# A cross-attention and expert block on one core: a new order of the same instructions on every engine, and a new bank table

## The reference

```python
# attention, on the normalised x
q = proj(_layernorm(x), Wq, bq); k = proj(ctx, Wk, bk); v = proj(ctx, Wv, bv)
scores = clip(einsum('bhsd,bhtd->bhst', q, k) / sqrt(32), -50, 50)
scores = clip(where(attend, scores, -10000.0), -50.0, 50.0)
probs = softmax(scores)
ctx = einsum('bhst,bhtd->bhsd', probs, v)
delta = clip(residual_scale, 0, 0.3) * (ctx @ Wo.T + bo)
x = x + layernorm(delta) * ln_gamma + ln_beta
# experts, on the normalised new x
logits = einsum('bth,eh->bte', _layernorm(x), router_w)
gate = softmax(logits) * top2_mask
h = silu(einsum('bth,eih->beti', _layernorm(x), down_w))
x = x + einsum('beth,bte->bth', einsum('beti,ehi->beth', h, up_w), gate)
```

## Time and profile before

| | us |
|---|---|
| median of 3 runs | 198.33 (197.42 to 199.66) |
| the profiled execution, device time | 198.77 |
| its span, first to last instruction | 197.1 |
| PE busy in it | 178.3 (90%) |
| DVE, ACT, POOL busy | 143.6, 112.5, 104.5 |
| mean granted clock of PE | 0.963 |

### The profile page before, as it was taken

The page is one execution under the profiler, slowest core; times in us unless marked ns, Lnnn a source line. Parts: engine busy times, 40 slices in busy tenths (PEclk is TensorE's granted clock), DMA queues, the critical chain, the costliest instruction groups (busy, mean ns, idle before and its releaser), DMA issues. The chain is left out here.

```text
span 197.1 us, 3587 instructions
## 1 busy us (share of the span) xinstructions
PE 178.3 (90%) x1228; PEld 130.7 (66%) x1228; DVE 143.6 (73%) x306; ACT 112.5 (57%) x231; POOL 104.5 (53%) x157
## 2 busy tenths in 40 slices
PE   7999999399993999999599999986999999999970
PEld 7777686258832587885286876663775977888840
DVE  2867799999845894056982606789698999678991
ACT  3038537778309685175666833589554868567500
POOL 4060035499969999388694111794244872472000
PEclk9999999969998599999889999999999999999998
DMA  5994994005694326773305401553434482002337
GB/s 165 358 388 143 292 398 181 0 7 226 176 254 147 78 91 190 174 192 127 110 0 189 139 10 39 192 211 110 119 106 157 155 276 73 0 2 106 136 130 271
DMA packets 18050, 30.14 MB, mean 153 GB/s; under 512 B 3056, under 2 KB 8176, under 8 KB 17776
## 3 DMA queue, kind: packets, MB, share of 16 engines
q1 hardware_dynamic: 18032, 29.92, 46.6%
HBM read 19.95 MB, written 9.96 MB: 152 GB/s over the span
## 5 line engine op out<-in xcount | busy, mean ns | idle before, releaser
L471 PE MATMUL ps<-hst_hi,wq_hi 128*128 128x512 f32 x64 | 27.4, 428 | 0.0
L471 PE MATMUL ps<-hst_hi,wq_lo 128*128 128x512 f32 x64 | 26.4, 413 | 0.0
L471 PE MATMUL ps<-hst_lo,wq_hi 128*128 128x512 f32 x64 | 26.4, 412 | 0.0
L471 PE MATMUL ps<-wo_hi,attt_hi 128*128 128x512 f32 x64 | 26.1, 407 | 0.0
L471 PE MATMUL ps<-wo_hi,attt_lo 128*128 128x512 f32 x64 | 25.3, 395 | 0.0
L471 PE MATMUL ps<-wo_lo,attt_hi 128*128 128x512 f32 x64 | 25.2, 394 | 0.0
L1510 POOL TENSOR_TENSOR attt_lo<-wk,attt_hi 128x512 fp32r<-128x512 f32 x16 | 23.3, 1471 | 1.5 <-ACT attt_hi L802 1.5
L1506 POOL TENSOR_TENSOR xs<-xs,beta_bc 128x512 f32<-128x512 f32 x16 | 21.4, 1366 | 2.2 <-DMA beta_bc<-beta 2.2
L862 ACT ACTIVATE cen<-xs,n_sum 128x512 f32<-128x512 f32 x16 | 11.5, 721 | 15.5 <-DVE xs L1175 15.5
L1148 DVE TENSOR_SCALAR stage<-stage,exp_max 128x1024 f32<-128x1024 f32 x16 | 19.0, 1205 | 2.0 <-ACT stage L784 1.8
L765 ACT ACTIVATE hs<-xs,ln_bias,ln_rstd 128x512 f32<-128x512 f32 x16 | 12.1, 808 | 13.2 <-POOL ln_bias L1498 13.2
(11 more groups left out here) (111 smaller groups left out, 396.9 us busy)
## 6 DMA issues: line engine op xcount, KB each, us to landing
wk<-rz_scratch SPq DMA_DIRECT2D x32, 128.0 KB, 2.7
out<-xs SPq DMA_DIRECT2D x16, 256.0 KB, 2.3
xs<-x SPq DMA_DIRECT2D x3, 1024.0 KB, 7.8
x_scratch<-x_turned SPq DMA_DIRECT2D x6, 512.0 KB, 2.6
x_turned<-x_scratch SPq DMA_DIRECT2D x24, 128.0 KB, 2.7
hs_scratch<-hs_turned SPq DMA_DIRECT2D x2, 1024.0 KB, 3.8
hs<-hs_scratch SPq DMA_DIRECT2D x8, 256.0 KB, 5.2
wk<-wk_t SPq DMA_DIRECT2D x4, 256.0 KB, 5.9
```

The costliest lines, as they stand in the source:

```text
L471: last = pe.matmul(dst, w, m, start=start and i == 0, stop=stop and i == n - 1, skip_group_check=unseen)
```

## The change

No function is changed and no instruction is added or removed, but for how adjacent ones group: the calls in the blocks of SP, PE, ACT, DVE and POOL stand in another order, and `BANKS` has other lines. The order of the start (loads, keys, values, batch 0's `query`) stays. Of the bank table one line:

```diff
-    "V0 h11 s00 v01 m0 s10 v11 s20 v21 f00 f02 a00 v30 v33 f12 f21 n30 f30 a21 a31",
+    "V0 h11 m0 v01 s10 s11 v12 s20 f01 f02 v22 v30 a01 f10 f12 f21 n31 f23 n32 a21",
```

SP, from the first transfer after the loads:

```diff
-            hs_send(2)
             spread_out(0, 0)
             spread_in(0, 0)
-            hs_fetch(2)
-            load(3)
             spread_out(0, 1)
             spread_in(0, 1)
+            hs_send(2)
+            hs_fetch(2)
+            spread_out(1, 0)
+            load(3)
+            spread_in(1, 0)
+            spread_out(1, 1)
+            x1_send(0, 0)
+            spread_in(1, 1)
+            x1_fetch(0, 0)
             hs_send(3)
+            x1_send(0, 1)
             hs_fetch(3)
```

```diff
+            x1_transpose(3, 3)
+            up(2, 0)
+            down(3, 2)
+            up(2, 1)
             hid_transpose(2, 1)
-            x1_transpose(3, 3)
-            down(3, 2)
             down(3, 3)
-            up(2, 0)
-            up(2, 1)
             hid_transpose(3, 0)
             up(2, 2)
             up(2, 3)
+            up(3, 0)
             hid_transpose(3, 1)
-            up(3, 0)
```

DVE and POOL:

```diff
             centre_wo(0)
             centre_wo(1)
+            centre_wo(2)
             tile_stats(2, 0)
             tile_stats(2, 1)
-            scale_gamma()
             tile_stats(2, 2)
-            tile_stats(2, 3)
-            clip(0, 0)
             hs_lo(1, 0)
             hs_lo(1, 1)
             hs_lo(1, 2)
+            clip(0, 0)
+            hs_lo(1, 3)
+            tile_stats(2, 3)
             clip(0, 1)
...
+            batch_power(1)
             up_low()
-            batch_power(1)
+            wo_low(0)
+            wo_low(1)
             add_beta(0, 0)
             add_beta(0, 1)
-            batch_power(2)
             add_beta(0, 2)
             add_beta(0, 3)
             add_beta(1, 0)
+            batch_power(2)
+            wo_low(2)
             add_beta(1, 1)
             add_beta(1, 2)
```

More of the change, by code:

```diff
@@ L644, in _ @@
             hs_transpose(1, 2)
+            scores(0, 0)
             hs_transpose(1, 3)
+            expert_means()
             scores(0, 1)
+            query(1, 0)
             sums(0, 0)
[L648 removed]
             query(1, 1)
[L650 to L651 removed]
             sums(0, 1)
@@ L986, in _ @@
+            hs_hi(3, 3)
+            x1_out(0, 2)
+            projected_squares(1, 3)
             x1_squares(1, 2)
-            projected_squares(1, 3)
+            x1_out(0, 3)
+            exp_scores(2, 2)
+            down_scaled(0, 1)
+            hidden_tanh(0, 0)
+            x1_squares(1, 3)
+            exp_scores(2, 3)
+            query_out(3, 0)
+            x1_out(1, 0)
+            x1_out(1, 1)
+            query_out(3, 1)
+            down_scaled(0, 2)
+            exp_logits(0, 0)
@@ L1402, in _ @@
             x1_turn(1, 1)
+            clip(2, 1)
             scaled(1, 2)
             residual(1, 2)
+            scaled(1, 3)
+            reciprocals(2, 0)
+            x1_turn(1, 2)
+            residual(1, 3)
+            x1_turn(1, 3)
+            clip(2, 2)
+            clip(2, 3)
             product(2, 0)
             product(2, 1)
-            x1_turn(1, 2)
+            largest(0, 0)
+            gating(0, 0)
+            reciprocals(2, 1)
+            largest(0, 1)
+            gating(0, 1)
+            clip(3, 0)
+            clip(3, 1)
             product(2, 2)
-            scaled(1, 3)
-            residual(1, 3)
-            x1_turn(1, 3)
             product(2, 3)
-            clip(3, 0)
-            largest(0, 0)
-            clip(3, 1)
-            gating(0, 0)
             reciprocals(3, 0)
@@ L1419, in _ @@
             clip(3, 3)
-            largest(0, 1)
+            scaled(2, 0)
             hid_lo(0, 0)
-            reciprocals(3, 1)
-            scaled(2, 0)
-            residual(2, 0)
-            gating(0, 1)
-            scaled(2, 1)
-            residual(2, 1)
-            x1_turn(2, 0)
-            x1_turn(2, 1)
-            hid_lo(0, 1)
-            scaled(2, 2)
             product(3, 0)
             product(3, 1)
+            scaled(2, 1)
+            reciprocals(3, 1)
+            hid_lo(0, 1)
+            residual(2, 0)
+            x1_turn(2, 0)
+            residual(2, 1)
+            x1_turn(2, 1)
+            scaled(2, 2)
             residual(2, 2)
             x1_turn(2, 2)
+            scaled(2, 3)
             product(3, 2)
-            product(3, 3)
-            scaled(2, 3)
-            finish(0, 0)
             residual(2, 3)
@@ L1442, in _ @@
             largest(1, 0)
-            largest(1, 1)
+            product(3, 3)
+            finish(0, 0)
             finish(0, 1)
             finish(0, 2)
+            finish(0, 3)
             gating(1, 0)
+            largest(1, 1)
+            hid_lo(1, 0)
             gating(1, 1)
+            scaled(3, 0)
+            residual(3, 0)
             largest(2, 0)
-            finish(0, 3)
-            scaled(3, 0)
-            hid_lo(1, 0)
             hid_lo(1, 1)
-            residual(3, 0)
             gating(2, 0)
```

426 lines of the change are left out of this document (198 added, 228 removed), and 14 rows, old and new, of the table BANKS.

## The result

The changed kernel took **190.5 us** in the median of 4 runs (190.36 to 192.76), against 198.26 (197.42 to 199.66, 4 runs) for the kernel before: ratio 0.9629, 95% interval 0.9538 to 0.9719. The forecast was 190.5 us. The profiled execution took 190.64 us with a span of 188.8 us; the mean granted clock was 0.989, and 0.963 before. Executions that took over 1.5% more than the fastest of their kernel are left out of all medians, ranges and intervals here (for after_both these were four at 191.22 to 192.2 us with mean granted clocks of 0.98 to 0.986, while its other two had 1.0 and 0.998), and the profiles of after_two_stores and before_no_beta, which are of such executions, serve only to place waits.

A forecast was written before the change was run, and what follows sets the result against it. TensorE, busy 90% of the 197.1 us span, was taken as the bound. Removing 16.6 us of waits and clock loss gave 180.5; 8.7 of new waits made 189.2 of span, 190.5 us after run offsets; range 185.5 to 197.

The forecast's parts named there:

- The base: TensorE's old waits, 11.3 us, plus clock loss, 5.3 us: 16.6 us can go, leaving a floor of 180.5 us span.
- Place A: Batch-1 projection, TensorE waiting for hst_lo: 1.8 us (1.2 to 3.4) replaces 3.2 + 0.9; no clock loss.
- The clips: Three early VectorE clips, possibly delayed by GpSimd, hold weigh(0, 0): 0 to 2.0 us of wait, taken as 0.9.
- Place B: ScalarE held behind batch 2's DRAM transfer: 6.2 us go; the next late chain, reciprocals' broadcast, taken as 0 (0 to 2.0).
- The front of the projections: project(0, 0) waits for two GpSimd att_lo: 0 to 2.9 us, taken as 1.8 including weigh(1, 0)'s small wait.
- `weigh(3, 0)`: Batches 2 and 3: it waits for two products behind a 7.4 us reciprocal spread; 0 to 2.0, taken as 1.1 us.
- The end and the small waits: New alternation of the last up, hid_transpose and down: 1.2 us (0 to 2.5); other small waits 0.6.
- The tail: Last up, finish adds and stores, ending at 197.1 us: counted as something that can't go.
- (1): Rival: new waits hide one another, about a third of 8.7 us left; 184.7 us, chance 0.15.
- (2): Rival: waits at project(0, 0) or weigh(3, 0) pass some 2 us and lower the clock; about 194 us, chance 0.18.
- (3): Slower rival: reciprocal spreads through DRAM take 11 us or more and become the bound; about 203 us, chance 0.09.
- (4): Rival: clips and residuals meet GpSimd as often as before; 193 us, chance 0.08.

The follow-up runs named there:

- after_both: Changed kernel with the edits of after_lo_first and after_bo_late together; 188.27 us from two executions, no interval.
- after_two_stores: Changed kernel with each half's reciprocals stored to DRAM twice, one store behind the other; 196.56 us, ratio 0.9877 to the kernel before.
- before_no_beta: Kernel before without GpSimd's sixteen adds of ln_beta (ln_beta missing from the output); 195.92 us, ratio 0.9862 to the kernel before.
- after_lo_first: Changed kernel with batch 1's low parts on VectorE ahead of three of batch 2's statistics; 187.33 us, ratio 0.9471 to the kernel before.
- before_exp_first: Kernel before with query_out(1, 3) and batch 1's first two exponentials ahead of batch 2's four hs_hi on ScalarE; 200.18 us, ratio 1.0127.
- after_bo_late: Changed kernel with centre_bo moved behind product(0, 3) on VectorE; 189.44 us, ratio 0.953 to the kernel before.
- before_lift_lo: Kernel before with batch 1's low parts (VectorE) and tile (1, 3)'s high part (ScalarE) moved ahead of batch 2's steps; 200.87 us, ratio 1.0128.

## Why the prediction came out as it did

**The base was right.** The old stretch less the waits and clock of before is 184.1 - 16.6 = 167.5 us. The changed kernel's rows of waits give 8.4, and the lowered clock 1.5 (below): 177.4, which is what was measured. For after_lo_first, 167.5 and its rows of 1.8, 1.7, 1.3, 0.9, 0.9, 0.7, 0.5 and 0.3 us give 175.6, against 175.5. That the sum of waits plus clock accounts for PE's time held in both.

**Place A**: taken as 1.8 us, measured 2.44, inside its bounds but above the 1 to 2 us that the prediction named as its sign. "I take no clock loss here" failed. The `scores` took 2.01 for 1.11 us and `query(1, 0)` 3.64 for some 3.05 (43.34 to 46.98): 1.5 us. after_lo_first got both wait and clock back, 3.1 us, of which 1.9 are left in its stretch, as small waits of up to 1.0 us appeared elsewhere. The kernel's old order itself was uneven here: the same wait was 3.23 us in its profile and 1.65 in that of before_exp_first, which has the same steps up to there. In the second PE came 0.4 us later and DVE 1.2 us earlier, 0.9 of that by one `centre_wo` of 0.49 us in place of 1.42; why they differed stays open. The step on the clock rested on one counter-example, 1.6 us without a loss, for a wait whose own bound was 3.4.

**The clips**: 0.9 was taken at `weigh(0, 0)`, where it was 0: only one of the first four took over 1 us (1.14). The delay came one batch later, where no term stood: `clip(1, 0)` and `clip(1, 1)` took 3.45 us together beside GpSimd's `att_lo` and `wo_low`, and `sums(1, 0)` waited 1.40. The mechanism was right and its place wrong. after_bo_late took that wait away and had no shorter stretch, as the clock fell behind the next wait.

```profile
59.69 3.45 DVE L1148 TENSOR_SCALAR stage<-stage,exp_max 128x1024 f32<-128x1024 f32 x2
```

The Trainium skill, page "SBUF — State Buffer", section "Who interferes with whom", says that such an instruction and one of GpSimd exclude each other. The trace agrees at this place: 1.73 us a clip where the best is 0.65. The reading by which no clip would be delayed and the term would be 0 was wrong here.

**Place B** was right in its two halves: the 6.2 us went, and 0 was taken for the chain to `scores(1, 1)`, where PE's timeline shows no wait. That this place can't be won by ACT's order alone was not in the working; before_exp_first showed it.

**The front of the projections**: 1.8 taken, 1.65 measured. **`query(2, 0)`**: 0.8 taken, 0 measured. **`weigh(1, 1)`**: 0.5 taken, 0.37 measured. **`weigh(3, 0)`**: 1.1 taken, 1.36 measured, on the named chain. **The end and the small waits**: 1.8 taken; the rows for `hidt_lo` and for `xs` come to 1.0.

**The tail was taken as unchanged**, "the last `up` ... and the stores end at 197.1", 5.9 us, and was 3.4. DVE's adds behind the last `up` account for 0.8 of it (192.65 - 191.15 = 1.5 before, 186.17 - 185.45 = 0.7 now), since four and not six stand in a row. The rest lies behind the last add, where the old order also gave 2.9 us (before_lift_lo) and the new one 4.5 (after_lo_first); SP's wait for the last `out` was 2.1 us in the first of these and 3.7 in the second.

So 1.8 us there are not the change's. They and the 0.8 offset the clock (1.5) and the later start (1.0): the forecast's agreement to 0.1 us is in part luck, while its stretch, 184.1 - 16.6 + 8.7 = 176.2, was 1.2 us short of the 177.4.

**Rivals.** (1) didn't come: the waits summed to what was listed. (2) came at place A and not at the two places that it named: 0.6 us more of wait and 1.5 of clock, the low end of its 2 to 5, which the shorter tail and the smaller terms offset. (3) see after_two_stores. (4) was partly true: the residuals were as slow as before (915 against 882 ns) and the clips faster (998 against 1205), and what this is worth in time isn't shown. Not tried: one engine's whole new order with the others' old, and the new bank table by itself. So the runs show that the place of the send and of the projections is needed for the gain, but not what share of it the bank table has.

## What to carry to other kernels

Read a wait's releaser back through its own queue before moving it: the row named ACT's exponentials, but the transfer behind them was the bound, and each of three local repairs in the old order made the kernel slower. Put the longest independent block of the bounding engine's work over a round trip through DRAM, and only then move the producers' steps forward. Compare kernels by the bounding engine's stretch between fixed instructions; here the first and last microseconds of an execution varied by as much as one term of the sum.
